# Last product, layer norm and store moved into the edge loop of a two-layer graph network

## What is computed

```python
def _L1_gnn_ref(x, edge_index, edge_attr, timestamps, We1, be1, We2, be2, Wt, bt, Wn1, bn1, Wn2, bn2):
    ts = timestamps[:, None]
    ef = jax.nn.relu(edge_attr @ We1 + be1) @ We2 + be2
    tw = jax.nn.sigmoid(ts @ Wt + bt)
    ef = ef * tw
    row, col = (edge_index[0], edge_index[1])
    combined = jnp.concatenate([x[row], ef], axis=1)
    msg = jax.nn.relu(combined @ Wn1 + bn1) @ Wn2 + bn2
    out = jax.ops.segment_sum(msg, col, num_segments=x.shape[0])
    return out + x
...
x = _layernorm(x + _L0_gnn_ref(x, L0_gnn_w1, L0_gnn_w2, L0_gnn_a, src, dst), axis=-1)
x = _layernorm(x + _L1_gnn_ref(x, edge_index, edge_attr_64, edge_weight, ...), axis=-1)
```

## Time and profile before

| | us |
|---|---|
| median of 3 runs | 2329.46 |
| lowest, highest | 2328.28, 2330.48 |
| profiled execution, its own time | 2327.27 |
| span of its trace | 2325.5 |

### The profile page before, as it was taken

One profiled execution on the slowest core, in us unless ns is written; L12 is line 12 of the kernel. 1 busy time (PEld: TensorE's weight loads), 2 busy tenths in 40 slices (PEclk: granted clock), 3 DMA queues, 4 the chain that ended last, 5 costly groups with the idle time before them and its releaser, 6 DMA issues.

```text
span 2325.5 us, 45201 instructions
## 1 busy us (share of the span) xinstructions
PE 2007.7 (86%) x12672; PEld 1317.7 (57%) x12673; DVE 1235.8 (53%) x2842; ACT 663.7 (29%) x1433; POOL 1610.2 (69%) x1692
## 2 busy tenths in 40 slices
PE   6589888899898898898778889988998989898884
PEld 5366666665666665666555555555555555555553
DVE  5455555555555555555465555555555555555555
ACT  5111111111111111111143333434343434334344
POOL 4677777777777777777006777777777777777771
PEclk9698989997989988989778999999999999999997
DMA  7532232223322223232125554545545455545442
GB/s 193 140 82 84 83 82 83 80 78 83 83 83 82 76 82 82 83 82 64 31 74 150 127 133 128 132 128 132 132 128 133 127 133 127 132 128 132 129 114 67
DMA packets 251926, 245.45 MB, mean 106 GB/s; under 512 B 143119, under 2 KB 189200, under 8 KB 251886
## 3 DMA queue, kind: packets, MB, share of 16 engines
q1 hardware_dynamic: 197214, 134.38, 21.1%
q0 software_dynamic: 53648, 109.59, 18.9%
q10 hardware_dynamic: 1024, 0.98, 0.2%
HBM read 229.77 MB, written 10.27 MB: 103 GB/s over the span
## 4 chain that ended last, share of the span: by engine, by line
PE 34%; POOL 27%; issue 23%; DVE 7%; DVEq 2%; DMA 2%; ACT 1%; POOLq 1%; SPq 0%; ACTq 0%
POOL T L605 26%; PE ps L1354 9%; PE ps L1346 7%; PE ps L1339 7%; PE ps L1389 5%; PE ps L1393 3%; DVEq L1002 2%; DVE R L1053 1%; DVE E L995 1%; ACT V L720 1%; POOL G L572 1%; DVE XM L1057 1%; DMA T<-in_x 1%; DVE st L1075 1%; PE ps L1413 1%
## 5 line engine op out<-in xcount | busy, mean ns | idle before, releaser
L605 POOL DMA_INDIRECT T<-y_rows,idx x832 | 793.9, 954 | 373.3 <-issue 370.6
L572 POOL DMA_INDIRECT G<-hi_rows,idx x832 | 806.0, 969 | 282.9 <-issue 262.5
L1486 PE MATMUL ps<-G 128*128 128x64 f32 x1664 | 229.2, 281 | 101.8 <-ACT G L794 99.3
L1339 PE MATMUL ps<-ident,G 128*128 128x128 f32 x832 | 204.2, 333 | 126.9 <-DVE XM L1057 45.9
L794 ACT ACTIVATE G<-G 128x512 f32<-128x512 f32 x208 | 131.0, 630 | 616.0 <-DVE G L1180 616.0
L995 DVE TENSOR_TENSOR E<-ps,V 128x512 f32<-128x512 f32 x208 | 142.6, 686 | 287.7 <-ACT V L720 286.7
L1486 PEld LDWEIGHTS ps<-G 128*128 128x128 f32 x1664 | 203.3, 192 | 151.2 <-ACT G L794 122.4
L1180 DVE TENSOR_TENSOR G<-ps,T 128x512 f32<-128x512 f32 x208 | 143.8, 691 | 261.8 <-DMA T<-y_rows,idx 259.8
L720 ACT ACTIVATE V<-ps 128x512 f32<-128x512 f32 x208 | 124.3, 598 | 545.7 <-PE ps L1346 544.3
L1354 PE MATMUL ps<-E,AwP 128*32 128x128 f32 x1940 | 252.7, 302 | 10.4 <-DVE E L995 10.3
L1339 PEld LDWEIGHTS ps<-ident,G 128*128 128x128 f32 x832 | 117.0, 160 | 217.2 <-issue 215.1
(11 more groups left out here) (147 smaller groups left out, 2231.7 us busy)
## 6 DMA issues: line engine op xcount, KB each, us to landing
T<-in_edge_weight SPq DMA_DIRECT2D x207, 256.0 KB, 3.5
Dbc<-block_destinations SPq DMA_DIRECT2D x69, 384.0 KB, 3.6
T<-in_edge_attr SPq DMA_DIRECT2D x207, 128.0 KB, 2.4
G<-hi_rows,idx POOLq DMA_INDIRECT x832, 2.6
T<-y_rows,idx POOLq DMA_INDIRECT x832
T<-in_x SPq DMA_DIRECT2D x12, 448.0 KB, 6.8
link<-scan_destinations SPq DMA_DIRECT2D x70, 56.4 KB
y_rows<-T SPq DMA_DIRECT2D x7, 448.0 KB, 3.2
```

Source lines behind the costliest of these rows:

```text
L572: pool.indirect_dma_start(out=G[:, s, t * C:(t + 1) * C], out_offset=None, in_=hi_d[:, :], in_offset=bass.IndirectOffsetOnAxis(ap=idx[:, s ...
L605: pool.indirect_dma_start(out=Yb[:, r, t * C:(t + 1) * C], out_offset=None, in_=y_d[:, :], in_offset=bass.IndirectOffsetOnAxis(ap=idx[:, r ...
L1339: pe.matmul(U[j][:, i * P:(i + 1) * P], G[:, s, t * C:(t + 1) * C], ident[:, :], is_transpose=True, start=(i == 0), stop=False, skip_group ...
L1486: ins = pe.matmul(ps[4][:, 0:W], hS[:, i * C:(i + 1) * C], ohB[:, i * W:(i + 1) * W], start=(i == 0), stop=(i == 3))
```

## The change

In the fast path, blocks 0 to 45 (`LOOPED` = 46) are finished inside the edge loop, one per turn, and blocks 46 to 48 behind it. Block m is finished in turn k = m + 7 (`LAG`). `run_edges` gets a second hardware loop for the turns from 7 on. In the calls of such a turn:

- r = 0: ScalarE copies the 128 columns of block m from `accH` to `aF`;
- r = 1: TensorE multiplies `aF` with `wN2`, into `ps[5]`;
- r = 2: VectorE adds X1 (`finish`) and takes the statistics;
- r = 3: VectorE aggregates them, makes the reciprocal root of the variance by a shift, a subtraction and three Newton steps (`scale`; twelve small operations, each of which waits for the one before it), and normalises (`normalise`);
- SyncE stores the block at the head of the next turn, ahead of the turn's loads.

ScalarE's root, reciprocal and normalise of the last layer norm are gone from the fast path. The slow path keeps the seven chunks. The flag `unusual` now is also set when a block would not be complete at its copy.

```diff
+LAG = 7
+NEWTON = 11
+LOOPED = NQ // RB + 1 - LAG
...
             for q in range(2 * RB):
-                edge(q, q % RB, q // RB)
-            with eng.Fori(2, NQ // RB - 1) as k:
+                edge(q, q % RB, q // RB, None)
+            with eng.Fori(2, LAG) as k:
                 for r in range(RB):
-                    edge(k * RB + r, r, k)
+                    edge(k * RB + r, r, k, None)
+            with eng.Fori(LAG, NQ // RB - 1) as k:
+                for r in range(RB):
+                    edge(k * RB + r, r, k, k - LAG)
             for q in range(NQ - RB, NQ + 4):
-                edge(q, q % RB, q // RB)
+                edge(q, q % RB, q // RB, q // RB - LAG)
...
+                def store(m):
+
+                    sp.wait_ge(s_f["x1"], m + 1)
+                    sp.dma_start(out[bass.ds(m * P, P), :], yF).then_inc(s_out[0], 16)
...
+                with sp.Fori(LAG + 1, NQ // RB - 2) as k:
+                    store(k - LAG - 1)
+                    for r in range(RB):
+                        load(k * RB + RB + r, r)
...
+                    if r == 0 and m is not None and (not is_int(m) or m < LOOPED):
+                        act.wait_ge(s_b["acc"], (m + LAG - 1) * RB)
+                        need(act, s_f["o"], m)
+                        act.activation(aF, accH[:, bass.ds(m * P, P)], ACT.Copy).then_inc(s_f["copy"], 1)
...
+            settled(dve.tensor_scalar(first, iotaF[0:1, 0:LOOPED], float(P), float(P), ALU.mult, ALU.add))
+            settled(dve.tensor_tensor(ahead, first, baseR[0:1, (LAG - 1) * RB:(LAG - 1 + LOOPED) * RB:RB], ALU.is_gt))
+            settled(dve.tensor_reduce(late[:, 0:1], ahead, AX.X, ALU.add))
+            settled(dve.tensor_tensor(late[:, 1:2], late[:, 0:1], ps[7][0:1, 0:1], ALU.add))
+            dve.tensor_scalar(unusual[:, :], late[:, 1:2], 1.0, None, ALU.min).then_inc(s_flag, 1)
...
+                def finish(m, n, o, x1, xf, yf):
+
+                    dve.wait_ge(s_f["o"], m + 1)
+                    dve.tensor_tensor(xf, x1, o, ALU.add).then_inc(s_f["xs"], 1)
+                    dve.wait_ge(s_f["xs"], m + 1)
+                    passed(dve, "dve")
+                    for i in range(n):
+                        ins = dve.bn_stats(st[:, i, :], xf[:, i * C:(i + 1) * C])
+                    ins.then_inc(s_f["st"], 1)
+
+                def scale(m, n):
+                    dve.wait_ge(s_f["st"], m + 1)
+                    passed(dve, "dve")
+                    for i in range(n):
+                        ins = dve.bn_aggr(mv[:, 0, i, :], st[:, i, :])
+                    ins.then_inc(s_f["mv"], 1)
+                    dve.wait_ge(s_f["mv"], m + 1)
+                    v, y, t = ve[:, 0, 0:n], rs[:, 0, 0:n], sd[:, 0, 0:n]
+                    left = [0]
+
+                    def seen(ins):
+                        left[0] += 1
+                        ins.then_inc(s_f["nr"], 1)
+                        dve.wait_ge(s_f["nr"], NEWTON * m + left[0])
+                    seen(dve.tensor_scalar(v, mv[:, 0, 0:n, 1], EPS, None, ALU.add))
+                    seen(dve.tensor_scalar(t.bitcast(I32), v.bitcast(I32), 1, None, ALU.arith_shift_right))
+                    seen(dve.tensor_scalar(y.bitcast(I32), t.bitcast(I32), -1.0, float(0x5f3759df), ALU.mult, ALU.add))
+                    for i in range(3):
+                        seen(dve.tensor_tensor(t, y, y, ALU.mult))
+                        seen(dve.scalar_tensor_tensor(out=t, in0=t, scalar=-0.5, in1=v, op0=ALU.mult, op1=ALU.mult))
+                        ins = dve.scalar_tensor_tensor(out=y, in0=t, scalar=1.5, in1=y, op0=ALU.add, op1=ALU.mult)
+                        if i < 2:
+                            seen(ins)
+                    ins.then_inc(s_f["rs"], 1)
+
+                def normalise(m, n, xf, yf):
+                    dve.wait_ge(s_f["rs"], m + 1)
+                    for i in range(n):
+                        ins = dve.tensor_scalar(yf[:, i * C:(i + 1) * C], xf[:, i * C:(i + 1) * C], mv[:, 0, i, 0:1],
+                                                rs[:, 0, i:i + 1], ALU.subtract, ALU.mult)
+                    ins.then_inc(s_f["x1"], 1)
...
+                    if m is not None and (not is_int(m) or m < LOOPED):
+                        if r == 2:
+                            dve.wait_ge(s_x2, m + 1)
+                            finish(m, 1, ps[5][:, 0:C], X1[:, bass.ds(m, 1), :].rearrange("p b c -> p (b c)"), xF, yF)
+                        if r == 3:
+                            scale(m, 1)
+                            need(dve, s_out[0], 16 * m)
+                            normalise(m, 1, xF, yF)
...
+                    if r == 1 and m is not None and (not is_int(m) or m < LOOPED):
+                        pe.wait_ge(s_f["copy"], m + 1)
+                        need(pe, s_f["xs"], m)
+                        pe.matmul(ps[5][:, 0:C], aF, wN2[:, :], start=True, stop=True).then_inc(s_f["o"], 1)
                 run_edges(pe, edge)
                 pe.wait_ge(s_b["acc"], NQ)
...
+                for i in range(rest):
+                    n0 = (LOOPED + i) * P
+                    ins = pe.matmul(ps[6][:, i * C:(i + 1) * C], accH[:, n0:n0 + P], wN2[:, :], start=True, stop=True)
                 ins.then_inc(s_f["o"], 1)
```

More of the change, by code:

```diff
@@ L776, in _ @@
                     act.activation(hR, zR, ACT.Relu).then_inc(s_3["h"], 1)
+                for c in range(NC):
+                    deviation(c, s_f)
+                    need(act, s_out[c % 2], 16 * (c // 2))
+                    scale_rows(c, s_f, xs[c % 2], yS[c % 2])
             with act.Else():
@@ L1477, in _, with edge @@
                 pe.wait_ge(s_3["back"], NB + 1)
+                for c in range(NC):
+                    need(pe, s_f["xs"], c - 1)
+                    for i in range(NCH):
+                        n0 = (c * NCH + i) * P
+                        ins = pe.matmul(bank(2 * (c % 2), i), accH[:, n0:n0 + P], wN2[:, :], start=True, stop=True)
+                    ins.then_inc(s_f["o"], 1)
             with pe.Else():
-                def edge(q, r, k):
+                def edge(q, r, k, m):
                     g4, z, e, h, t = (later(q, lag) for lag in (4, 3, 2, 1, 0))
```

83 lines of the change are left out of this document (46 added, 37 removed).

## The result

| | us |
|---|---|
| before, median of 4 runs | 2328.87 (2322.76 to 2330.48) |
| changed, median of 4 runs | 2393.99 (2385.89 to 2396.04) |
| ratio, 95% interval | 1.0287, 1.0263 to 1.0311 |
| changed: profiled execution, its span | 2394.49, 2392.8 |

The change costs 65 us, where 12.7 were forecast and the range ended at 2368. The span grew from 2325.5 to 2392.8, by 67.3 us.

What follows compares the result with a forecast made beforehand. GpSimd's queue was taken to bound the loop at 20.14 us a turn, the tail second. Tail -27.3 us and loop +40 us over 44 turns gave +12.7: 2340 us profiled, 2342 on the median, range 2301 to 2368.

Steps and rivals of the forecast that it cites:

- Direction and bound: Edge loop: GpSimd's 20.14 us turn gives way to TensorE with VectorE's chain at 21.05; slower, chance 0.55.
- the signs named: Edge loop: turn about 21 us, TensorE idle some 2 us once a turn, clock near 0.92, GpSimd waiting for free buffers.
- The tail: Behind the last add into `accH`: 12.4 us left of 39.7, giving back 27.3 us.
- The chain at r = 3: VectorE's last quad of a turn: 6.29 us from transposes to `hS` product, TensorE idle 2.04 us, turn 19.48 us.
- The clock: TensorE behind the idle: half clock in nine turns of ten, 1.75 us lost each, 1.57 us a turn.
- the forecast's own case: Edge loop: turn 20.9 to 21.9 us, time 2334 to 2378 us; chance 0.52.
- rivals 3 and 4: Edge loop: balanced turn 20.7 to 20.9, 2325 to 2334 us, chance 0.09; turn 20.9 to 21.9, 2334 to 2378, chance 0.52.
- Rival 1: Edge loop: GpSimd stays the bound, turn 20.14 us, only the tail counts, 2302 us; chance 0.23.
- Rival 5: Edge loop: VectorE's new operations slow three gathers, 0.76 us a turn, GpSimd's turn 20.9, time 2335 us; chance 0.04.
- Nothing for product, copy, sum, statistics and store: Edge loop: these moved operations cost nothing, TensorE's product being 0.26 us and sum and statistics 0.3 us each.

Runs made afterwards that it cites:

- `i3_root1`: Changed kernel with one Newton step in place of three in the root, six small operations fewer: 2298.26 us beside 2323.02 of the kernel before.
- `h2_spread`: Changed kernel with the block's layer-norm chain spread over five quads, on a stalled chip; the three stalled runs took 3345.03, 3341.55 and 3355.19 us.

## Why the prediction was wrong

- **Direction and bound: right.** GpSimd set the pace; now TensorE behind VectorE's chain does, by the signs named: the gap once a turn, released by ScalarE's ReLU, GpSimd waiting for buffers, VectorE for TensorE. Two of the signs came out worse than named: a granted clock of 0.87 in place of 0.92, and a turn of 22.36 us in place of 21.
- **The tail: right.** 12.4 us forecast behind the last add, 11.4 measured, so 28.3 gained and not 27.3. Three normalises take 0.86 us, three aggregates 0.31, and from the end of the last normalise at 2389.25 the stores and their landing take 3.55 us, less than the 4.7 taken.
- **The chain at r = 3: right.** Root steps at 0.19 to 0.20 us. From the copy's start to the aggregate's 2123.83 - 2117.43 = 6.40 us against 6.26 by the sum. The branch, which showed in no row: from the last normalise's start at 2120.62 to L1264 are 1.45 us, against 1.36 taken; the part of it that was put down to the jump, 0.35 us, is seen in no run by itself. The gap is 2.18 against 2.04 us, the full-clock turn 19.7 against 19.48.
- **The clock: the step that failed.** "I take nine turns in ten with a slow stretch: 1.57 us". The stretch came in 43 of 43 turns, which is +0.18; but the size was taken from one event of the trace of before, behind a gap of 1.02 us, in which one stretch cost 1.75 us. Behind 2.2 us, 19 of 43 turns have slow stretches of twice or four times that length, and the mean cost is 2.6 us by the turns' lengths, 2.77 by half the slow time. Of the 1.31 us by which a turn is longer than forecast (22.36 against 21.05) about 1.1 are this term's and 0.2 the chain's. No rival held such a thing: the forecast's own case ended at a turn of 21.9. With 2.77 in place of 1.57 the sum is 19.48 + 2.77 = 22.25 us a turn, 44 x 2.11 = +93, less 27.3: 2395 us, 1 us from the measured time; that it comes so near is in part luck, since 2.77 is a little too much and 19.48 a little too little. The times of rivals 3 and 4 were reckoned from 2327.27 and those of the other rivals from 2329.5; the 2 us between change nothing here.
- **Rival 1, GpSimd stays the bound (2302): wrong here, but it is the kernel without the fall.** The filled and the spread kernel took 2294 and 2297 us. Its condition, a slow clock in fewer than four turns of ten, is what they meet: none and eight of 43 turns.
- **Rival 5, GpSimd slowed by VectorE: refuted.** L630 takes 950 ns in the mean against 954 before, with the new operations beside it, and its issue takes 164.9/574 = 0.29 us against 0.30; in the filled and the spread kernel 956 and 954. By rival 5's 0.76 us a turn the mean of the sixteen gathers would have risen by 0.05 us, to about 1000 ns. The rule of the Trainium skill, SBUF — State Buffer, section Who interferes with whom, shows no effect on this kernel's gathers.
- **Nothing for product, copy, sum, statistics and store: borne out as a whole.** With all of them in the loop and the clock up, the turn is 20.15 to 20.19 us, against 20.14 before. ScalarE's copy stands behind the ReLU that ends the gap (2124.35 and 2123.15), so it doesn't make it; a kernel with the copy alone was not run to an answer.

The Trainium skill, TensorE: Matmul & The Clock Gate, section HAM oscillation — how this bites in real kernels, counts the cost of falls as the slow time times one half, in a kernel whose clock falls anew in each turn of its loop. The trace nearly agrees: 5.5 us of slow time a turn are 2.77 us by that rule, and by the turns' lengths the loss is 22.36 - 19.7 = 2.6 us.

## What to carry to other kernels

When work is put on one engine's path, add up not only whether it fits under the bound but how long a single gap it opens on TensorE. Here one gap of 2.2 us in each turn cost more through the clock behind it (2.6 us) than the chain itself, which would have been hidden (a turn of 19.7 us under 20.14). The length of the gap is a sign and not a threshold: gaps of 2.0 to 2.25 us were followed by a fall every time, shorter ones now and then. Spread a chain of small dependent operations over several pieces of the pipeline, or put idle products in the gap; the first turned +2.8% into -1.3%, the second into -1.5% in its one undisturbed run. And take the cost of a fall from gaps of the length that the change will make; where the trace has only shorter ones, the range must reach to several slow stretches on end.

## What the runs showed that was not expected

- More work took less time: 1.88 us more of matmuls a turn made the turn 2.17 us shorter, and the loop's clock 1.00 where the kernel before has 0.97.
- Behind gaps of 2.0 to 2.25 us, always at the same place of the turn, the slow stretch was 3.4, 6.8 or 13.7 us long. What picks the length is not settled; turns of 21.34 and 22.9 us mostly alternate.
- The clock also falls where no gap is longer than 1.64 us, and that costs next to nothing while TensorE has 1.6 us of slack a turn: 14 falls in 43 turns of `i3_root1`, and a mean turn of 20.18 us.
- On some chips all engines stall between instructions, the granted clock of the attention stage is 0.74 to 0.76 (0.56 in the trace of `h2_spread`) and not 0.88 to 0.90, and the kernel takes 3320 to 3400 us. What stalls them is open; a difference of 3% in this loop vanishes there.
